# Value products of a key tile moved between two rounds of score and maximum matmuls, in the attention stage of a four-stage kernel

## The reference

```
scores  = einsum('bkgsd,bktd->bkgst', qh, kh) / 4     # 8 key heads, 4 query heads on each, 16 dims
weights = softmax(scores, axis=-1)                    # over 512 keys
out     = einsum('bkgst,bktd->bkgsd', weights, vh)
```

## Time and profile before

| | |
|---|---|
| three runs | 2032.77, 2035.28, 2039.09 us, median 2035.28 |
| profiled execution, its own time | 2037.96 us |
| its span in the profile | 2036.1 us |
| mean granted PE clock | 0.879 |
| stage C | from about 730 to 1152 us of the span |

### The profile page before, as it was taken

How to read it: one execution, slowest core, us unless ns; L and a number is a source line. 1 busy time by engine, 2 the same in 40 slices (tenths; PEclk the granted TensorE clock), 3 DMA queues, 4 the chain that set the end, 5 groups by cost and what they waited for, 6 DMA issues and landing times.

```text
span 2036.1 us, 25086 instructions
## 1 busy us (share of the span) xinstructions
PE 1600.3 (79%) x7951; PEld 1063.5 (52%) x7952; DVE 980.0 (48%) x1543; ACT 703.3 (35%) x1117; POOL 673.8 (33%) x428
## 2 busy tenths in 40 slices
PE   4333578788877549999998761999999999999980
PEld 2222345354545324333333360787878888788870
DVE  2788565656556358888888420222221222222214
ACT  2343344353534217777776510111111111111110
POOL 1322051423314313131314225466276152720006
PEclk7666689899989759999999855999999999999995
DMA  7020000000000044444542036144043040420007
GB/s 281 1 83 0 21 1 0 0 0 0 0 0 0 21 109 124 131 140 139 168 144 68 4 132 238 39 150 155 31 155 144 31 155 31 155 103 31 31 21 247
DMA packets 74989, 166.98 MB, mean 82 GB/s; under 512 B 6834, under 2 KB 8371, under 8 KB 74291
## 3 DMA queue, kind: packets, MB, share of 16 engines
q1 hardware_dynamic: 58578, 129.01, 18.9%
q10 hardware_dynamic: 11232, 20.45, 2.9%
q0 software_dynamic: 5120, 16.78, 2.5%
HBM read 112.74 MB, written 52.95 MB: 81 GB/s over the span
## 4 chain that ended last, share of the span: by engine, by line
PE 58%; issue 14%; DVE 10%; POOL 9%; DMA 4%; ACT 3%; SPq 1%; POOLq 0%; DVEq 0%; ACTq 0%
PE psum L1595 9%; PE psum L1597 9%; PE psum L1596 9%; PE psum L1403 6%; DVE neg_max L1089 5%; PE psum L1429 4%; PE psum L1513 4%; PE psum L1502 3%; PE psum L1475 3%; POOL expert_weight_parts L682 3%; PE psum L1439 2%; PE psum L1366 2%; DMA w_of_even_expert<-in_L_ffn_w 1%; POOL normed_all L672 1%; PE psum L1619 1%
## 5 line engine op out<-in xcount | busy, mean ns | idle before, releaser
L1089 DVE TENSOR_REDUCE neg_max<-psum 128x2 f32<-128x1024 f32 x256 | 300.3, 1220 | 79.4 <-PE psum L1475 79.1
L849 ACT ACTIVATE probabilities<-psum 128x512 f32<-128x512 f32 x512 | 272.1, 600 | 86.5 <-PE psum L1502 81.5
L1595 PE MATMUL psum<-expert_weight_parts,sorted_tokens_t_first 128*128 x624 | 250.6, 402 | 10.6 <-POOL expert_weight_parts L682 7.5
L1597 PE MATMUL psum<-expert_weight_parts,sorted_tokens_t_second 128*128 x624 | 246.1, 394 | 0.0
L1596 PE MATMUL psum<-expert_weight_parts,sorted_tokens_t_first 128*128 x624 | 245.8, 394 | 0.0
L1206 DVE TENSOR_TENSOR expert_inner<-psum,expert_inner 128x512 f32<-128x512 f32 x78 | 53.9, 692 | 386.8 <-ACT expert_inner L885 386.8
L1475 PE MATMUL psum<-key_rows,query_rows 48*128 48x512 f32 x512 | 165.1, 502 | 29.5 <-DMA query_rows<-query_rows_of_units 18.4
L885 ACT ACTIVATE expert_inner<-psum 128x512 f32<-128x512 f32 x78 | 46.6, 598 | 396.9 <-PE psum L1597 396.9
L1502 PE MATMUL psum<-query_rows,key_rows 50*128 50x512 f32 x512 | 177.1, 443 | 6.8 <-ACT probabilities L849 3.7
L1513 PE MATMUL psum<-probabilities,value_and_one 128*32 128x512 f32 x1024 | 140.3, 621 | 0.0
L1595 PEld LDWEIGHTS psum<-expert_weight_parts,sorted_tokens_t_first 128*128 128x128 f32 x624 | 119.0, 191 | 36.9 <-issue 12.4
(11 more groups left out here) (225 smaller groups left out, 2874.7 us busy)
## 6 DMA issues: line engine op xcount, KB each, us to landing
w_of_odd_expert<-in_L_ffn_w SPq DMA_DIRECT2D x8, 2048.0 KB, 9.3
wo_of_expert<-in_L_ffn_wo SPq DMA_DIRECT2D x7, 2048.0 KB, 8.6
query_rows<-query_rows_of_units SPq DMA_DIRECT2D x64, 192.0 KB, 4.3
w_of_even_expert<-in_L_ffn_w SPq DMA_DIRECT2D x6, 2048.0 KB, 12.0
sorted_x<-zero_rows SPq DMA_DIRECT2D x13, 768.0 KB, 4.5
sorted_tokens<-sorted_x ACTq DMA_DIRECT2D x39, 256.0 KB, 2.7
sorted_y<-expert_out ACTq DMA_DIRECT2D x39, 256.0 KB, 2.1
query_rows_of_units<-dims_first SPq DMA_DIRECT2D x32, 256.0 KB
```

Source lines behind the costliest of these rows:

```text
L849: nc.scalar.activation(prob[t % 2][:, i * SEQ:(i + 1) * SEQ], bank[4 + n % 3], ACT.Exp, scale=HD ** -0.5).then_inc(c_e, 1)
L1089: nc.vector.tensor_reduce(of_pair[:, p, st, :], ring(("max", (m, i))).rearrange("p (h n) -> p h n", h=2), AX.X, ALU.max, negate=True).then ...
L1595: nc.tensor.matmul(out_bank, hi[:, cols], w_r[:, bass.ds(w_at, 512)], start=start, stop=False)
L1597: return nc.tensor.matmul(out_bank, lo[:, cols], w_r[:, bass.ds(w_at, 512)], start=False, stop=stop)
```

## The change

The call of `attend` moves into the loop over p and runs at p = 0. PE then issues the value products of the key tile before between the first and the second round of pairs, instead of after the second. Nothing else is changed: not the number of instructions, nor the list of ring jobs, nor the other engines' programs.

```diff
@@ attention(u), on PE
                             if there(u + 2):
                                 maximum(u + 2, 2 * t + p, 1 - h, h == 0)
-                    k = ST * u + t - 1
-                    if 0 <= k < ST * UNITS and (there(u) or t == 0):
-                        attend(k)
+                        k = ST * u + t - 1
+                        if p == 0 and 0 <= k < ST * UNITS and (there(u) or t == 0):
+                            attend(k)
                     if t == 0 and there(u + 1):
                         neg_max_transposed(u + 1)
```

## The result

The changed kernel took 2088.51 us (median of 6 runs, 2075.11 to 2100.31) against 2034.03 (6 runs, 2030.99 to 2039.09): a ratio of 1.0263, 95% interval 1.0217 to 1.031. Two things are to be explained: 54 us more, and a spread of 25 us where the kernel before had 8. The profiled execution took 2075.11 us, span 2073.3, and is the fastest of the six; it lies 37 us above the profiled execution of before.

What follows compares the result with a forecast made beforehand. Bound taken: PE and DVE handing two ring slots back and forth, beside an exponential loop. 34.5 + 2.4 + 4 + 2 - 1.3 = +41.6 us on the 2035.3 median gave 2077 us (68%); range 2044 to 2108, about 80%.

Steps and rivals of the forecast that it cites:

- Part 1: Steps with a ring job: 3.75 us between value products, against 3.16 (NEG), 3.36 (ATT) and 3.25 (chunk).
- The unknown term: Slot filled behind the products, m2 to its reduction's start: 0.81 us, bounds 0.4 and 1.2; ends -31 and +30 us.
- Part 2: Steps without a ring job: products wait for the previous tile's last exponential, 2.67 us against 2.61 to 2.67; +0.05 taken.
- Parts 3 and 4: ACT's sum copy at t = 0 costs nothing under 3.75 us steps; queueing behind a blocked `attend` is inside the step lengths.
- The sum for units 1 to 25: Units of 12.84 us, 13.92 with chunk: 338.3 less 303.8 is +34.5; statistics of units 9, 17 and 25 add +2.4.
- Units 26 to 29: No chunk, +4.0; shorter stalls of DVE's cast -2.4; products at 1.2 GHz +2.5; together +4 us.
- +2 for unit 0: Unit 0 runs at 1.2 GHz with products of 1.93 us: +2 us.
- -1.3 for two units: Units 30 and 31 have no maxima; ATT and NEG fall in ACT's shadow there: -1.3 us.
- rival A: PE's clock drops, for half of the 100 steps in units 1 to 25: +45 us more, 2122 us; 8%.
- B: Faster: plain steps bound by two reductions, 2.28 us; 46 to 48 steps x 0.33 gives -16, 2019 us; 8%.
- C: No change: DVE's 1.5 us idle a unit takes up the slots' delay; time within 6 us; 8%.
- D: Slower by little: one of three ring steps keeps its old length; half the sum, about 2055 us; 8%.

Runs made afterwards that it cites:

- keep_busy: Changed kernel plus three matmuls with overwritten results ahead of the ring job in key tiles 0 and 1 of units 0 to 29; 2077.74 us, ratio 1.0227.
- plain_only: Against the kernel before, value products moved between the rounds only in key tiles that no ring job follows; 2049.97 us, ratio 1.0083.
- ring_only: Against the kernel before, value products moved between the rounds only in key tiles that a ring job follows; 2061.41 us, ratio 1.0146.
- second execution: Changed kernel run again unchanged, for a second profile and more runs; 2088.55 us, ratio 1.0289 against the kernel before.
- maxima_first: Changed kernel with the second round's two maxima put ahead of the value products, its two scores left behind them; 2053.18 us, ratio 1.0111 against the kernel before.

## Why the prediction was right, point by point

- **What bounds the old order.** I read a hand-over of two slots between PE and DVE beside a loop over the exponential. Both are confirmed: shorter reductions gain 11.0 us in units 1 to 25 of the old order (15 by the medians, between two heaps of runs), and once they are short its steps are 2.87, 3.20, 3.26 and 2.61, PE's own loop.
- **Part 1, ring steps at 3.75.** Measured 3.75 (NEG) and 3.73 (ATT and chunk). The unknown term, m2 to the start of the reduction, was taken as 0.81 out of 0.4 to 1.2; it measured 0.79 (M3 at 1087.62, 1.79 behind the products, which hold PE for 1.00). The step with NEG came to 3.75 by a coincidence: M7's late reduction, the two operations that split the maxima, and M0's reduction leave DVE free for M1 just when M1 is filled, so that both paths end together.
- **Part 2, plain steps at 2.67.** Measured 2.67. Three of the four DVE gaps that I expected before the odd jobs came, 0.3 to 0.4 us each; M1 followed M0 without one. s3 no longer waits for an exponential, but s1 does: at 1081.59, 0.05 after the end of s2's exponential of the tile before, and 0.49 ahead of the products. The waits of scores for ACT went from 17.7 to 104.5 us in units 1 to 25 (time in which the value products run is counted in). So the bank loop of the old plain step did not go away; it moved to s1 and is as long as the path that I priced, to within 0.1 us.
- **Parts 3 and 4.** ACT's copy ended 0.65 us before the products of t = 1 in unit 24 (1084.58 + 0.60 against 1085.83) and cost nothing.
- **The sum for units 1 to 25**, 34.5 + 2.4 = 36.9. At full clock: in the first execution unit 2 took 19.63 us against 14.37 in `keep_busy`, and unit 3 0.66 more than its like, so 346.0 - 5.9 = 340.1, which is 36.3 above 303.8. That I came so near the profiled execution as a whole (2079.6 forecast, 2075.11 measured) is partly luck: 5.9 us of clock in these units, which the sum did not have, were more than made up by the 10 us that the stretches outside units 1 to 29 were shorter. `plain_only` and `ring_only` add up to +40 over the whole kernel, against my 41.6, with what little clock they lost counted in.
- **Units 26 to 29**: +4 forecast, +4.9 in this execution, and here the clock has the larger share: by an estimate, 0.81 against 0.88 is some 10 us more at 1.2 GHz, of which a third is lost. In the second execution unit 28 took 19.4 us. The +2 for unit 0 can't be seen: what lies before unit 1 was shorter. Unit 30 went from 11.63 to 11.25 us, in the direction of my -1.3 for two units.
- **What was mis-sized: rival A.** "My longest new wait is about 1.0 us" left out the units in which POOL holds up DVE ahead of NEG, at 2, 10 and 18; the weight loads' wait there was 1.76 us in unit 10. The clock did fall, not for half of the 100 steps but in one place (first execution) or four (second) of units 1 to 25, and in units 26 to 29 for longer than in the kernel before (24 and 31 us at 1.2 GHz, against 14). So forecast and rival A came true together. By medians the loss was 54 to 57 us: about 40 by the slots (the sum of the two halves), and the remaining 14 to 17 by the clock. An estimate from the runs' mean clocks agrees: 0.872, the middle of the first six runs, instead of about 0.881 in the kernel before is some 50 us more at 1.2 GHz, and a third of that is 17. I had put the two as alternatives. My 2077 us was for the slots alone and lies 11 us under the measured 2088.5.
- **B, C and D** fell with the step lengths; `plain_only` was the direct test of B. One slip: forecast and D make up at most 76% and not the 80% that I gave the range.
- The rule of the Trainium skill ("TensorE: Matmul & The Clock Gate", section "Why this matters for your kernels") is that idle gaps between bursts put PE back to half rate. The page speaks of longer gaps than those ahead of the falls in units 1 to 25. The runs agree with it only in part: the clock fell in the order with more waiting, but behind waits of 0.7 to 1.8 us, and a wait of 1.78 us in unit 18 left it at 1.00.

## What to carry to other kernels

Long work of one engine belongs where the engine that reads its results has two buffers filled; moved between the fills, it is paid at each hand-over, here 0.4 to 0.6 us beside the steps that I costed, 76 times. That is not enough by itself: with both fills ahead, the products could still close a longer loop over the score banks, as in `maxima_first`. To cost such a move, write the loop from one long piece of work to the next, with the waits that close it, once for a plain turn and once for each kind of extra job; such a count gave 36.9 us for 36.3 at full clock. And where PE starts to wait a little everywhere, allow for its clock as an addition and not as an alternative, and look first at the turns in which another engine already delays it: three of the four falls in units 1 to 25 of the second profile were there.

## What was not expected

- The time at half clock explains the spread. The six first runs stand in the order of their mean granted clock: 0.882 gave 2075, 0.876 2081, 0.874 2083, 0.870 2094 and 2096, 0.865 2100 us. As an estimate, from 0.882 to 0.865 is some 77 us more at 1.2 GHz (2 x 2098.5 x 0.135 less 2 x 2073.3 x 0.118); a third of it is 26 us, and the spread is 25.
- A step at 1.2 GHz takes 5.59 instead of 3.74 us, or 4.07 instead of 2.67: about a third of the half-clock time is lost.
- With three score banks the old place of the products has the shortest plain loop of the four tried: 2.61 against 2.67 (between the rounds) and 2.84 (ahead of the last score, and ahead of the last two).
